# The order of TensorE's products in the expert units of a recurrence-and-experts layer

## The reference

```
k, v, r = token-mixed xn times Wk, Wv, Wr           # r through a sigmoid
rwkv    = running, numerically safe weighted mean of v with exp(k), along each of 4 sequences of 512
s       = (r * rwkv) @ Wo.T
y       = sum over the 4 best of 16 experts e of  weight[t,e] * (silu(xn @ Wg[e]) * (xn @ Wu[e])) @ Wd[e]
out     = x + s * silu(y)
```

## Time and profile before

| | us |
|---|---|
| median of 3 runs | 346.5 (344.99 to 347.97) |
| the profiled execution | 347.63 |
| its span, first to last instruction | 345.7 |
| TensorE busy with matmuls | 299.8 (87%) |
| VectorE busy | 253.4 (73%) |
| GpSimd busy | 225.5 (65%) |
| ScalarE busy | 153.3 (44%) |

### The profile page before, as it was taken

One profiled execution on the slowest core, in us unless ns is written; L12 is line 12 of the kernel. 1 busy time (PEld: TensorE's weight loads), 2 busy tenths in 40 slices (PEclk: granted clock), 3 DMA queues, 4 the chain that ended last, 5 costly groups with the idle time before them and its releaser, 6 DMA issues.

```text
span 345.7 us, 4753 instructions
## 1 busy us (share of the span) xinstructions
PE 299.8 (87%) x1413; PEld 236.0 (68%) x1414; DVE 253.4 (73%) x498; ACT 153.3 (44%) x236; POOL 225.5 (65%) x223
## 2 busy tenths in 40 slices
PE   0798999797999999999999999999999999799000
PEld 0334444345888888888888888888888888588000
DVE  2879899859589597795995959959687010189992
ACT  1891864224644635628247273463652323172220
POOL 3500399948767777777777777777777724257363
PEclk9999999998999999999999999999999999999755
DMA  7894000043656557656475666656465698587132
GB/s 236 279 392 191 1 0 1 8 131 89 177 175 207 159 172 232 215 146 205 144 254 141 211 171 203 208 195 186 153 211 171 216 361 302 194 280 238 43 121 91
DMA packets 31723, 61.46 MB, mean 178 GB/s; under 512 B 4620, under 2 KB 22029, under 8 KB 31568
## 3 DMA queue, kind: packets, MB, share of 16 engines
q10 hardware_dynamic: 6848, 21.26, 19.8%
q1 hardware_dynamic: 17360, 21.24, 18.1%
q0 software_dynamic: 7488, 18.63, 17.3%
HBM read 48.52 MB, written 14.42 MB: 182 GB/s over the span
## 4 chain that ended last, share of the span: by engine, by line
PE 68%; DVE 12%; POOL 9%; DMA 6%; issue 3%; POOLq 0%; ACT 0%; ACTq 0%; DVEq 0%
PE ps L545 60%; POOL ohB L334 8%; DVE arena L983 5%; PE ps L650 5%; DMA rows<-y_rows 3%; PE ps L555 2%; DMA wrou<-wrouT_in 1%; DVE arena L998 1%; POOL arena L352 1%; DMA arena<-xn_rows,tok_idx 1%; DVE arena L758 1%; DVE rows L733 1%; DMA y_rows<-arena,e_idx 1%; DVE vT L767 1%; DVE rows L814 0%
## 5 line engine op out<-in xcount | busy, mean ns | idle before, releaser
L545 PE MATMUL ps<-arena,rows 128*128 128x256 f32 x624 | 142.8, 383 | 2.4 <-issue 2.4
L545 PEld LDWEIGHTS ps<-arena,rows 128*128 128x128 f32 x624 | 116.8, 192 | 17.2 <-issue 3.0
L352 POOL DMA_INDIRECT arena<-xn_rows,tok_idx x78 | 83.5, 1070 | 27.6 <-issue 21.0
L359 POOL DMA_INDIRECT y_rows<-arena,dst_idx x66 | 72.8, 1103 | 22.3 <-issue 19.8
L911 DVE TENSOR_TENSOR arena<-arena,ps 128x512 f32<-128x512 f32 x39 | 26.3, 675 | 65.7 <-PE ps L545 34.1
L545 PE MATMUL ps<-wdn,arena 128*128 x312 | 73.7, 380 | 0.0
L545 PEld LDWEIGHTS ps<-wdn,arena 128*128 128x128 f32 x312 | 59.3, 190 | 8.2 <-issue 0.3
L498 ACT COPY arena<-ps 128x512 f32<-128x512 f32 x39 | 22.8, 584 | 83.4 <-PE ps L545 83.4
L334 POOL TENSOR_SCALAR ohB<-late 128x128 f16<-128x128 f32 x24 | 30.7, 1291 | 24.9 <-DVE late L819 24.9
L545 PE MATMUL ps<-arena 128*128 128x512 f32 x96 | 45.5, 607 | 0.4 <-DVE arena L758 0.4
L493 ACT ACTIVATE arena<-ps 128x512 f32<-128x512 f32 x39 | 23.5, 602 | 27.5 <-PE ps L545 27.3
(11 more groups left out here) (140 smaller groups left out, 332.3 us busy)
## 6 DMA issues: line engine op xcount, KB each, us to landing
rows<-wgu_in ACTq DMA_DIRECT2D x39, 512.0 KB, 3.8
rows<-y_rows SPq DMA_DIRECT2D x3, 2048.0 KB, 11.1
wdn<-wd_in SPq DMA_DIRECT2D x1, 4096.0 KB, 14.4
rT<-x_in SPq DMA_DIRECT2D x4, 512.0 KB, 6.0
xn_rows<-rT SPq DMA_DIRECT2D x4, 512.0 KB, 3.6
kT<-x_in SPq DMA_DIRECT2D x8, 256.0 KB, 3.3
rows<-y_rows SPq DMA_DIRECT2D x8, 256.0 KB, 5.0
out<-arena SPq DMA_DIRECT2D x8, 256.0 KB, 2.1
```

The source lines that it names most:

```text
L352: pool.indirect_dma_start(out=xg[i % XG][:, j, :], out_offset=None, in_=xn_rows, in_offset=bass.IndirectOffsetOnAxis(ap=tok_idx[:, 2 * i + ...
L359: pool.indirect_dma_start(out=y_rows, in_=ysb[:, par, j, :], in_offset=None, out_offset=bass.IndirectOffsetOnAxis(ap=idx[:, n + j:n + j + ...
L545: ins = nc.tensor.matmul(dst, lhsT(c), rhs(c), start=(c == 0), stop=(c == C - 1))
```

## The change

TensorE's step becomes transposition i, down i-2, gate/up i: the gate/up product now follows the transposition of its own unit, with one down product between. The steps of ScalarE follow: in step i come the copy of x(i), the copy of y(i-2), the Exp if i is 1 modulo 4, the Silu of i, and the load of the weights of unit i+2. VectorE's products are the same and in the same order; only the place of a register read and of the last product moves into the common steps. The wait for the projections' buffers moves ahead of gate/up 0. After the last step only two down products remain. Their experts are read into registers before unit 31 on TensorE (`last_two`), and ScalarE reads two counts for its last two copies before unit 31 (`taken`), beside `blocks` and `low`, which it reads one unit earlier than before.

```diff
@@ ScalarE
             def step(i, blocks=None):
                 evac_x(i)
-                if i > 0:
-                    if i <= NEED and (i - 1) % HALF == 1:
-                        piece = (i - 1) // HALF
-                        act.wait_ge(args_ready, piece + 1)
-                        nc.scalar.activation(args, args, ACT.Exp).then_inc(exps_ready, 1)
-                    silu(i - 1, (i - 1) % 2)
-                    if i + 1 < NP:
-                        next_expert(i + 1, blocks)
                 if i > 1:
                     evac_y(i - 2, i % 2, 32 * ((i - 2) // 2))
-
-            for i in range(FIRST - 1):
+                if i < NEED and i % HALF == 1:
+                    act.wait_ge(args_ready, i // HALF + 1)
+                    nc.scalar.activation(args, args, ACT.Exp).then_inc(exps_ready, 1)
+                silu(i, i % 2)
+                if i + 2 < NP:
+                    next_expert(i + 2, blocks)
+
+            for i in range(FIRST - 2):
                 step(i)
             act.wait_ge(slots_known, 3)
             blocks, low = units_used(act)
-            step(FIRST - 1, blocks)
+            taken = [act.value_load(used[0:1, n:n + 1], min_val=32 * (NEED // 2 - 1), max_val=32 * (NP // 2)) for n in (4, 5)]
+            for i in (FIRST - 2, FIRST - 1):
+                step(i, blocks)
             optional(act, blocks, lambda i: step(i, blocks))
-            silu(low + LAG - 1, (FIRST - 1) % 2)
...
+            evac_y(low + LAG - 2, FIRST % 2, taken[1])
+            evac_y(low + LAG - 1, (FIRST - 1) % 2, taken[0])
@@ TensorE
             def step(i):
                 transpose_x(i)
-                if i > 0:
-                    gate_up(i - 1, (i - 1) % 2, 16 * ((i - 1) // 2 + 1))
+                if i == 0:
+                    pe.wait_ge(proj_out, BATCH * 3 * C)
                 if i == 2:
                     pe.wait_ge(wdn_in, 16)
                 if i > 1:
                     down(i - 2, i % 2, expert_of(i - 2))
+                gate_up(i, i % 2, 16 * (i // 2 + 1))
 
             pe.wait_ge(experts_ready, 1)
             for i in range(FIRST):
-                if i == 1:
-                    pe.wait_ge(proj_out, BATCH * 3 * C)
+                if i == FIRST - 2:
+                    blocks, low = units_used(pe)
+                    last_two = [expert_of(low + LAG - 2), expert_of(low + LAG - 1)]
                 step(i)
-            blocks, low = units_used(pe)
             optional(pe, blocks, step)
-            gate_up(low + LAG - 1, (FIRST - 1) % 2, 16 * blocks + 16)
-            down(low + LAG - 2, FIRST % 2, expert_of(low + LAG - 2))
-            down(low + LAG - 1, (FIRST - 1) % 2, expert_of(low + LAG - 1))
+            down(low + LAG - 2, FIRST % 2, last_two[0])
+            down(low + LAG - 1, (FIRST - 1) % 2, last_two[1])
@@ VectorE
-            for i in range(FIRST - 1):
+            for i in range(FIRST):
+                if i == FIRST - 1:
+                    blocks, low = units_used(dve)
                 step(i)
-            blocks, low = units_used(dve)
-            optional(dve, blocks, lambda i: step(i - 1))
-            hidden(low + LAG - 1, (FIRST - 1) % 2)
+            optional(dve, blocks, step)
```

## The result

| | before | after |
|---|---|---|
| median, us | 347.24 (4 runs) | 359.62 (4 runs, 358.65 to 360.63) |
| ratio | | 1.0381, 95% interval 1.0341 to 1.0421 |
| profiled execution, span | 345.7 | 358.7 |

What follows compares the result with a forecast made beforehand. TensorE was taken to set the pace at 5.62 us a unit. The terms 1.6 + 6.8 + 0.44 + 2.15 + 0.5 + 1.4 = 12.9 gave 360.5 profiled, 359.4 against the median; range 354.5 to 364.5.

Steps and rivals of the forecast that it cites:

- The stall in each piece: In each recurrence piece (four units), gate/up 4p+2 waits 0.97 us for ScalarE's copy behind the Exp; seven rounds cost 6.8.
- The first piece: At the start, VectorE's scan sets the first Exp; gate/up 0's earlier start is lost and 1.6 us added.
- The clock: TensorE's clock falls after the longest gap, in the first piece: 1.4 us, and 0 for gaps of 1 us.
- Register reads: Four ScalarE register reads ahead of the copy of x(31) stall TensorE once, about 2.1 us; 2.15 in the sum.
- Late weight loads: In steady units, weight loads issued late ahead of the copy exceed its 0.14 us margin: 0.5 added, ends 0 and 1.5.
- The drain: At the end, the jump out of the optional units stays and leaves the same 2.35 us gap; ends 0 and 4.
- Exp too early for a stall: Rival, not slower: arguments come 0.97 us earlier, no piece stalls, 345.3 in medians; chance 0.06.
- The clock did not fall at the gaps of 1 us: Rival: the clock falls in every piece, 1.4 us for each of seven more gaps, 370; chance 0.06.
- VectorE was not the bound: Rival: VectorE becomes the bound, Exp 9.36 us after gate/up 4, stall 2.58, 371 in all; chance 0.03.
- The stalls were not half as long: Rival: stalls as forecast but half as long, 350 to 355 us; chance 0.04.
- no steady gate/up started late: Rival: the wait is held in the sequencer, each gate/up starts 0.1 to 0.3 late, 4 to 11 us more; chance 0.03.
- The sum: All terms over the whole kernel: 12.9 us added to the profiled execution's 347.63, giving 360.5, or 359.4 against the median.

## Why the prediction was right

**The stall in each piece.** Right in place and size, with two errors that cancelled. From gate/up 4 to the Exp it took 7.86 (forecast 7.75): VectorE's gating product started 3.82 after the gate/up (at 110.76) and not 3.71, and the 4.04 behind it were exact. The table load had ended by then, at 114.64 (forecast 7.68 after gate/up 4, measured 7.70). From the Exp to gate/up 6 it took 4.34 (forecast 4.46): the matmul started 0.05 after the copy and not 0.14, which I had from a row at the start of the run. One thing I had not seen: a gate/up that starts after a stall takes 0.11 longer to the next transposition (119.14 to 122.70 is 3.56). So the loop is 4.34+11.24+0.11+7.86 = 23.55 against 23.45. The experiments that moved the Exp or lengthened what follows it show the cause.

**The first piece.** Right: VectorE's scan set the time of the first Exp, and the earlier start of gate/up 0 bought nothing. Relative to the scan gate/up 2 came 1.52 later, forecast 1.6. When the Exp no longer stood ahead of the copy, gate/up 2 came at 91.67 and 90.98 instead of 93.72: there the early start is real.

**The clock.** I took 1.4 behind the gap of 3 us and it cost 1.66, more than the 1.4 that I had as the most. That it fell in the profiled execution is partly luck: the same program up to that place had a gap of 3.06 in the run with the reads moved, and no loss. The second loss, 1.7 under the last down products, I did not forecast. It hardly shows in the end, because the scatters hid all but 0.2 of it.

**Register reads.** 2.03 against 2.15, shown by their removal. The prediction's own working gives this: four reads are 2.16, of which the margin of 0.14 hides a part, 2.02; the sum left the margin out.

**Late weight loads.** I added 0.5. In the profile after, 0.4 fall between gate/up 6 and 30 (6.79 less 6 times 1.07) and 0.56 behind unit 31 (1.00 less 0.44), of which 0.1 is the slower restart after the stall there; 0.8 to 0.9 in all. The term was too small, and its mechanism is shown by the run that moved the load. That it reached 2.1 us once the large stalls were gone, most of it behind the Exps, I had not worked out.

**The drain.** The jump did stay, and the measured branch of 6.16 us left a gap of 2.65 against 2.35. The branch is short when less code is skipped: 6.16 against 0.35 us. That is in line with the Trainium skill (Runtime: NRT & Kernel Launch, section Instruction fetch mechanics), which says that a taken branch to a target outside the fetched window has to wait for a fetch. The fetch itself as what ended the branch is not shown by these profiles. By the Trainium skill (ScalarE: Activation LUTs, section What ACT_TABLE_LOAD costs) each piece would have cost 1.38 more; the trace after again has 3.22 from Exp to Silu (114.80 to 118.02), so the table load costs 1.28 here and no more.

**The rivals.** None came. Exp too early for a stall needed 6.78 and it was 7.86. The clock did not fall at the gaps of 1 us, also not at those of 1.3. VectorE was not the bound, as the added copy arrived whole. The stalls were not half as long, and no steady gate/up started late: they follow each other 5.62 apart where nothing stands in the way.

**The sum.** That it met the profile to 0.1 us is luck. The stages for which I had forecast a change came to 13.98 against 12.9, by the 0.1 behind each stall, the late loads and the clock, and the stages for which I had forecast none to -0.98, of which -1.21 is the chance of the start. What was right is the mechanism and, within some 0.1 us each, the stall of every piece, the first piece and the reads.

## What to carry to other kernels

When a product is moved closer to the one that feeds it, count the slack in the helper's queue and not in the producer's: everything that stands ahead of the copy, also once in four steps, also a register read or a DMA issue, is now on the critical path. Putting those things behind the copy gave all the loss back without touching TensorE. A run-time branch that skips much code cost 2 to 3 us where it was exposed, and the reordering never won that much over the whole kernel; shorten what it skips, or put it where nothing waits.

## What the runs showed of the hardware

- A taken branch of TensorE's sequencer over four pairs of units took 3.83 to 6.16 us, in nine profiles; over one pair it took 0.35 to 0.36, in three.
- The clock does not follow the length of the gap alone. After 2.72, 2.98, 3.07 and 3.47 us the sixteen matmuls of gate/up 2 took 5.41, 5.28, 5.41 and 5.19, after 3.06 in the run with the reads moved 3.72. At the end a gap of 2.35 was followed by 3.82 and one of 2.33 by 5.40.
- A register read of ScalarE from on-chip memory took 0.53 us (265.6 to 267.7 for four), and the copy that stood behind the four, whose input was there at 264.96, started at 267.80.
